# SyncE's queue takes three of the four parts of each adjacency unit in the sweeps, ScalarE's queue one

## What is computed

```
e   = x with a scaled 64x64 product added (one weight for users, one for items)
h   = adj @ (adj.T @ e)                                  # layer 0
x1  = layernorm(x + layernorm_gamma_beta(h) + x)
T1  = adj @ x1
T2  = 2 * (adj @ T1) - x1                                # layer 1, Chebyshev recurrence
T3  = 2 * (adj @ T2) - T1
out = layernorm(x1 + x1 @ W0 + T1 @ W1 + T2 @ W2 + T3 @ W3 + bias)
```

## Time and profile before

| | us |
|---|---|
| three runs | 1209.78, 1214.84, 1215.15 |
| median | 1214.84 |
| the profiled execution, its own time | 1212.09 |
| its span, first to last instruction | 1210.2 |
| mean granted TensorE clock | 0.98 of full |
| HBM read | 348.97 MB, 289 GB/s over the span |

### The profile page before, as it was taken

One profiled execution on the slowest core, in us unless ns is written; L12 is line 12 of the kernel. 1 busy time (PEld: TensorE's weight loads), 2 busy tenths in 40 slices (PEclk: granted clock), 3 DMA queues, 4 the chain that ended last, 5 costly groups with the idle time before them and its releaser, 6 DMA issues.

```text
span 1210.2 us, 13868 instructions
## 1 busy us (share of the span) xinstructions
PE 1109.8 (92%) x5004; PEld 479.3 (40%) x5004; DVE 922.2 (76%) x960; ACT 332.1 (27%) x594; POOL 257.6 (21%) x420
## 2 busy tenths in 40 slices
PE   4999999999999997899889999999999999598794
PEld 3454445444444453444233333344344443122231
DVE  2698798999899898697777766665666667588783
ACT  1456456456466465300000000000100000011010
POOL 0476655464363453100000000000000000011111
PEclk9999999999999999899999999999999999798898
DMA  7999999999999987899999999999999999999991
GB/s 227 300 289 298 282 299 315 289 296 279 299 275 282 296 233 167 186 313 286 266 347 347 336 313 293 318 292 255 261 336 319 336 304 330 348 306 342 353 352 30
DMA packets 372730, 350.82 MB, mean 290 GB/s; under 512 B 11612, under 2 KB 371332, under 8 KB 372692
## 3 DMA queue, kind: packets, MB, share of 16 engines
q1 hardware_dynamic: 259092, 237.35, 70.5%
q10 hardware_dynamic: 110880, 110.11, 31.8%
q0 software_dynamic: 2720, 2.86, 0.9%
HBM read 348.97 MB, written 1.31 MB: 289 GB/s over the span
## 4 chain that ended last, share of the span: by engine, by line
PE 55%; SPq 12%; DVE 12%; ACT 10%; ACTq 5%; issue 4%; POOL 1%; DMA 1%; DVEq 0%; POOLq 0%
PE bank L1174 31%; ACT terms L774 9%; SPq L337 7%; ACTq L279 5%; SPq L326 4%; DVE turned L496 4%; PE bank L1225 4%; PE bank L1187 3%; PE bank L1044 2%; PE bank L1004 2%; PE bank L1032 2%; PE bank L1056 2%; PE bank L1016 2%; DVE shared L516 2%; PE bank L1203 1%
## 5 line engine op out<-in xcount | busy, mean ns | idle before, releaser
L1174 PE MATMUL bank<-turned,terms 128*128 128x512 f32 x680 | 301.4, 596 | 4.5 <-DVE turned L496 3.1
L386 POOL COPY raw<-raw 32x512 f32<-32x512 f32 x320 | 194.8, 609 | 243.6 <-DVE raw L533 205.1
L516 DVE STREAM_TRANSPOSE shared<-shared 32x512 f32<-32x512 f32 x320 | 224.0, 700 | 4.1
L1004 PE MATMUL bank<-shared 128*64 128x256 f32 x1600 | 206.1, 385 | 6.5 <-DMA shared<-in_adj 6.4
L496 DVE STREAM_TRANSPOSE turned<-raw 128x2048 f32<-128x2048 f32 x72 | 165.1, 2301 | 58.9 <-PE bank L1174 50.0
L496 DVE STREAM_TRANSPOSE turned<-shared 128x2048 f32<-128x2048 f32 x68 | 156.0, 2302 | 60.3 <-PE bank L1174 46.0
L774 ACT COPY terms<-terms 32x512 f32<-32x512 f32 x320 | 197.1, 616 | 5.1 <-DVE terms L526 0.9
L1174 PEld LDWEIGHTS bank<-turned,terms 128*128 128x128 f32 x680 | 126.6, 190 | 170.3 <-issue 164.0
L431 POOL DMA_DIRECT2D out<-scratch x40 | 21.7, 549 | 681.1 <-DVE scratch L724 681.0
L1004 PEld LDWEIGHTS bank<-shared 128*64 128x64 f32 x1600 | 111.6, 136 | 88.4 <-issue 33.1
L765 ACT COPY scratch<-bank 128x512 f32<-128x512 f32 x80 | 46.6, 585 | 131.2 <-PE bank L1016 130.9
(11 more groups left out here) (144 smaller groups left out, 1059.7 us busy)
## 6 DMA issues: line engine op xcount, KB each, us to landing
shared<-in_adj SPq DMA_DIRECT2D x100, 1024.0 KB, 10.7
raw<-in_adj SPq DMA_DIRECT2D x106, 512.0 KB, 10.6
raw<-in_adj ACTq DMA_DIRECT2D x106, 512.0 KB, 12.3
shared<-in_adj SPq DMA_DIRECT2D x104, 512.0 KB, 10.6
shared<-in_adj ACTq DMA_DIRECT2D x104, 512.0 KB, 12.1
raw<-in_adj SPq DMA_DIRECT2D x80, 256.0 KB, 7.6
xq<-in_x POOLq DMA_DIRECT2D x40, 32.0 KB, 6.2
out<-scratch POOLq DMA_DIRECT2D x40, 32.0 KB, 5.2
```

The source lines that it names most:

```text
L386: last = nc.gpsimd.tensor_copy(moved[Q32 * c:Q32 * (c + 1), :, :, Q32 * q:Q32 * (q + 1)], beside[Q32 * q:Q32 * (q + 1), :, c, :, :])
L516: last = nc.vector.transpose(low_turned[Q32 * c:Q32 * (c + 1), :, :, Q32 * q:Q32 * (q + 1)], low[Q32 * q:Q32 * (q + 1), :, :, Q32 * c:Q32 ...
L1004: last = nc.tensor.matmul(t_bank[H * odd:H * (odd + 1), 0:PW], e[:, s * SB + b, :], panels[slot][:, s * SB + b, :], start=(k == 0 and b < ...
L1174: last = nc.tensor.matmul(sum_bank[parity][:, :], terms[:, c * GB + i, columns], turned[place][:, i * BANK:(i + 1) * BANK], start=(first a ...
```

## The change

In each of the two loops over the units the list of parts is changed. SyncE's queue issues part 2, then 1, then 0; ScalarE's queue issues part 3 alone. Slots, waits, semaphore counts and the order of units stay.

```
@@ SyncE's loop
                 else:
                     sp.wait_ge(tile_turned, free_after(u) + 1 + RAW)
-                for q in (1, 0):
+                for q in (2, 1, 0):
                     load_part(sp, u, q)
@@ ScalarE's load_next
                 else:
                     act.wait_ge(tile_turned, free_after(u) + 1 + RAW)
-                for q in (3, 2):
-                    load_part(act, u, q)
+                load_part(act, u, 3)
                 issued[0] += 1
```

## The result

The changed kernel takes 1478.97 us (median of 4 runs, 1465.24 to 1491.69), the kernel before 1214.07. The ratio is 1.2149 (95% interval 1.2055 to 1.2244): slower by 265 us. The ratio is taken without the slowest of the four, which stands 1.8% above the fastest. The forecast was 1493 us, in a range of 1300 to 1565.

The account below looks back on a forecast made before the run. Loading and TensorE (92% busy) were taken as nearly level. 101 units at 9.5 us, 960 us in place of 681, add 279 to the 1210.2 us span: 1489, execution 1491, median 1493 us; 80% range 1300 to 1565.

Parts of the forecast that it names:

- the unit: Loading one unit (two tiles, four parts, 2.097 MB) in the changed kernel: 9.5 us, at 220 GB/s.
- all of it goes on the path: Over the sweeps, TensorE's 6.9 us and VectorE's 4.6 us lie beside 9.5 us of loading, so loading sets the time.
- The floor of 7.6 us: Shortest unit in the changed kernel: ScalarE's part entirely hidden, SyncE's three parts alone take 7.6 us; total 1299 us.
- The worst case of one part after the other: Changed kernel's unit without any overlap: 4 x 2.54 us = 10.2 us, +346 us, total 1558 us.
- The limit is of 32 partitions, not of a queue: In the loads, 203 GB/s limits a 32-partition part; one queue loading over 128 partitions reaches 348 GB/s.
- With the change the two queues start a unit with parts 2 and 3: At each unit's start both queues go to the same half; then SyncE sends 1 and 0 alone; 8.1 to 10.2 us.
- Two parts run side by side only if both queues issue at about the same moment: For the loads on both queues: overlap needs near-simultaneous issues, as happened twice per unit before the change; 3.01 us per pair.
- a part waits for the parts issued ahead of it, on whichever queue: Service follows issue order across both queues, read from two early ScalarE parts that landed 11.9 us after issue.
- Rival 1: ScalarE's part is hidden, or two parts of one half reach 348 GB/s: unit 7.6 to 8.1 us, 1300 to 1350; chance 0.28.
- Rival 2: SyncE's consecutive parts overlap as DMA engines drift apart: 6.3 to 7.6 us per unit, 1220 to 1300 us; chance 0.09.
- Rival 3: No rate lost, ScalarE freed around 1014.90 to 1052.10 us: up to 6 us faster, 1208; faster 0.05, within 0.5% 0.03.
- TensorE's clock: At 0.8 of full clock throughout, a unit costs TensorE 8.6 us, still under 9.5; nothing added to the sum.

Follow-up runs that it names:

- the pairs in step: Kernel before with SyncE parts 0, 2 and ScalarE 3, 1 (across halves) or 1, 3 (same half), plus a handshake before each part: 1278.18 and 1482.53 us.
- the run with part 2 last: Changed kernel with SyncE's parts in the order 1, 0, 2 in place of 2, 1, 0; ScalarE keeps part 3: 1450.64 us.
- the cross-half pairs: Kernel before with SyncE's parts 0, 2 and ScalarE's 3, 1, without handshake: 1442.41 us (four runs, 1387.38 to 1463.12).
- the run without part 3: Changed kernel without ScalarE's part, VectorE waiting for three parts, a quarter of each unit old data: 1274.8 us.

## Why the prediction was right

- **Direction and size.** 1493 forecast, 1479 measured; +279 us in the sum, +260 in the span. The mis-sized term is the unit: 9.5 us from 220 GB/s, measured 9.27 at 227. The count of 101 units held. So did "all of it goes on the path": +256 us come from the units.
- **The bounds.** The floor of 7.6 us for SyncE's three parts measured 7.2. The worst case of one part after the other (10.2 us, at 206 GB/s) was a little too high: all four on SyncE ran at 216 GB/s, 9.7 us.
- **The limit is of 32 partitions, not of a queue.** Shown by the pairs in step. The figure of eight ports in the Trainium skill ("SBUF — State Buffer", section "Door 1: The DMA port swizzle"), about 218 GB/s, is what the long single-queue windows have (216, 218). Its next section, by which two DMAs on two halves serialize with 6% gained, doesn't hold here: 287 against 222 GB/s, and 348 in the kernel before.
- **One step failed, and the number didn't hang on it.** "With the change the two queues start a unit with parts 2 and 3", and so meet in one half. They don't start together: ScalarE's part is issued 7.7 us ahead of SyncE's first one (median). By the packets part 3 moves beside part 2 of its own unit for 7 us in the whole run and beside any part 2 for 88 us, but beside part 0 for 168 us (243 GB/s) and beside part 1 for 41 us (267). So the collision in one half isn't what costs: SyncE's queue moves mostly alone for 503 of 870 us, at 220 GB/s, and the other half beside it brings little. The forecast gave two parts in different halves 348 GB/s, and by that ScalarE's part should have been hidden. The number stood because the sum took 9.5 us from one row of parts one after the other, and not from the collision. In this step it was luck. The run with part 2 last says the same: the first parts of the two queues lie in different halves there, and it gained 28 us, not 130.
- **A second was too narrow.** "Two parts run side by side only if both queues issue at about the same moment" left out that, with both queues full, it doesn't matter when they issue; what matters is that each keeps to its half. By that step the cross-half pairs should have been as fast as before; they were 230 us slower (175 in the fastest run). And "a part waits for the parts issued ahead of it, on whichever queue" is only roughly so: in the changed kernel ScalarE's part begins to move when 1.8 of SyncE's parts that were issued earlier have yet to move (median), and ends when they have all moved.
- **Rivals.** Rival 1 (ScalarE's part hidden) falls by the run without part 3: the part costs 2.1 us. Rival 2 (SyncE's consecutive parts overlap) is small in this order: 218 GB/s for SyncE's 2, 1, 0 alone against 216 for 0, 1, 2, 3. It is worth more where the halves alternate (261 in the best stretch). Rival 3 falls twice: ScalarE was freed wholly, as its issues show, and nothing came of it; and what could be had by getting its copies sooner, forecast as 6 us at best, turned out a loss of 30 in the form that was tried. The rule in the section "Issuing engines are not separate DMA queues" ("DMA: Bandwidth & Descriptors", the Trainium skill), by which the issuing engine doesn't matter to the transfers, doesn't hold here: with all parts issued by SyncE the kernel took 1528 us, with two parts on either engine 1214.
- **TensorE's clock.** 0.92 of full in sweeps 1 and 2 (503 to 1184 us) and 0.82 in sweep 3, above the 0.8 that was allowed for in the sum. TensorE held VectorE up for 25.5 us in all, against 402.7 us for data.

## What to carry to other kernels

If transfers cover only part of the partitions, look at which partitions move at the same moment, by windows in which one queue is alone: here 32 partitions alone or beside their own half gave about 215 GB/s, beside the other half up to 348 when both queues were full. Give each queue its own half of the partitions and an equal share: then a late issue on one of them costs only while that queue is empty. If the queues alternate halves, a late issue can put them in the same half for hundreds of us. A share of busy DMA engines near 1 says nothing about this, only bytes per time do. And a range that holds the result doesn't prove the story told with it: here the count and the rate held, and the reason given for the rate did not.

## What the runs showed of the hardware

- Two queues with level loads and each alternating between the halves ran anywhere between 213 and 290 GB/s within one execution, and the same kernel took 1387 to 1463 us in four runs, where the kernel before stays within 0.5%. Without a handshake the program doesn't set the phase between two queues, and it can be seen in the time.
- Both queues moving in different halves brought 329 GB/s on average in the kernel before, 306 with a handshake, 248 with three parts on one queue and one on the other. What makes the difference is not known.
- One queue alone, alternating its half every 256 KB, reached 259 GB/s on average over 750 us; in whole parts of 512 KB it went from 224 to 261 over some hundreds of us and back to 232.
- Of three parts, the same bytes took 1275 us on one queue and 1195 on two with a half each.
